# A state-space and layer-norm stage: loops unrolled, tables in halves, moments taken by ScalarE

## The reference, cut to what matters

```
dt  = exp(log_dt);  A = -exp(inv_A_real) + 1j * A_imag;  dtA = A * dt
Cc  = B * C * (exp(dtA) - 1) / A
K[c, h, l] = 2 * real(sum_n Cc[c, h, n] * exp(dtA[h, n] * l))       # c < 16, h < 128, n < 64, l < 1024
h   = K                                                            # 16 x 128 tokens of 1024 features
xn  = (h - mean(h)) / sqrt(var(h) + 1e-5)                          # over the 1024 features of a token
h   = h + attention(xn);   h = h + ffn(layernorm(h))
```

## Time and profile before

| | us |
|---|---|
| median of 3 runs | 2087.96 (2087.77 to 2090.44) |
| the profiled execution | 2088.66 |
| its span, first to last instruction | 2086.7 |
| PE busy in the span | 1896.5 (91%) |
| DVE busy | 1163.6 (56%) |
| POOL busy | 618.0 (30%) |
| ACT busy | 612.7 (29%) |
| mean granted TensorE clock | 0.978 |

### The profile page before, as it was taken

The page is one execution under the profiler, slowest core; times in us unless marked ns, Lnnn a source line. Parts: engine busy times, 40 slices in busy tenths (PEclk is TensorE's granted clock), DMA queues, the critical chain, the costliest instruction groups (busy, mean ns, idle before and its releaser), DMA issues.

```text
span 2086.7 us, 31307 instructions
## 1 busy us (share of the span) xinstructions
PE 1896.5 (91%) x13212; PEld 1029.0 (49%) x13212; DVE 1163.6 (56%) x1476; ACT 612.7 (29%) x869; POOL 618.0 (30%) x261
## 2 busy tenths in 40 slices
PE   0377699999999898878999999999999999999999
PEld 0367576666656554444554444444444444444444
DVE  8998547777777778855644544444444444210111
ACT  2154324334333334421112333333333333200000
POOL 2675013343333334433310322232232232011101
PEclk9998799999999999999999999999999999999999
DMA  2022211111132112135441321322322232533441
GB/s 90 10 71 60 65 35 33 39 39 35 29 94 72 27 36 60 57 104 194 154 147 61 119 94 62 101 91 61 101 91 77 85 101 72 195 120 116 142 142 41
DMA packets 99812, 173.32 MB, mean 83 GB/s; under 512 B 13984, under 2 KB 75168, under 8 KB 91744
## 3 DMA queue, kind: packets, MB, share of 16 engines
q1 hardware_dynamic: 99680, 171.41, 25.7%
HBM read 114.22 MB, written 56.11 MB: 82 GB/s over the span
## 4 chain that ended last, share of the span: by engine, by line
PE 73%; DVE 8%; POOL 2%; issue 2%; ACT 2%; DMA 1%; SPq 1%; ACTq 0%; DVEq 0%
PE acc L1194 14%; PE acc L1123 14%; PE acc L1124 14%; PE ps_p L930 3%; PE ps_p L931 3%; PE ps_p L932 3%; PE acc L1044 3%; PE acc L1045 3%; PE acc L1046 3%; PE ps_t L957 2%; PE ps_p L946 2%; PE ps_p L948 2%; PE ps_p L947 2%; DVE prob L1464 2%; PE ps_l L1139 2%
## 5 line engine op out<-in xcount | busy, mean ns | idle before, releaser
L1123 PE MATMUL acc<-x_hi,q_f 128*128 128x512 f16 x1376 | 522.0, 379 | 0.0
L1124 PE MATMUL acc<-x_lo,q_f 128*128 128x512 f16 x1376 | 521.5, 379 | 0.0
L1194 PE MATMUL acc<-down_levels,hid_parts 128*128 128x512 f16 x1376 | 300.1, 379 | 0.0
L890 POOL TENSOR_TENSOR prob<-prob,mx 128x1024 f32<-128x1024 f32 x64 | 121.4, 1897 | 421.9 <-DVE mx L1471 421.9
L1123 PEld LDWEIGHTS acc<-x_hi,q_f 128*128 128x128 f16 x1376 | 134.5, 98 | 174.8 <-issue 17.8
L899 POOL TENSOR_SCALAR q_f<-q_raw 128x2048 f16<-128x2048 int32 x22 | 121.1, 5504 | 316.3 <-PE acc L1124 315.4
L1194 PEld LDWEIGHTS acc<-down_levels,hid_parts 128*128 128x128 f16 x1376 | 133.2, 98 | 163.1 <-issue 5.0
L1124 PEld LDWEIGHTS acc<-x_lo,q_f 128*128 128x128 f16 x1376 | 134.7, 98 | 156.9
L930 PE MATMUL ps_p<-x_hi,w_qk 128*128 128x512 f16 x512 | 196.8, 384 | 0.0
L931 PE MATMUL ps_p<-x_lo,w_qk 128*128 128x512 f16 x512 | 196.0, 383 | 0.0
L932 PE MATMUL ps_p<-x_hi,w_qk 128*128 128x512 f16 x512 | 195.7, 382 | 0.0
(11 more groups left out here) (284 smaller groups left out, 3081.5 us busy)
## 6 DMA issues: line engine op xcount, KB each, us to landing
q_raw<-in_gu_q SPq DMA_DIRECT2D x22, 1024.0 KB, 7.1
hidden_parts<-hidden SPq DMA_DIRECT2D x42, 512.0 KB, 3.5
hid_parts<-hidden_parts SPq DMA_DIRECT2D x15, 1376.0 KB, 6.7
down_raw<-in_down_q SPq DMA_DIRECT2D x22, 512.0 KB, 5.1
w_raw<-in_w_qk SPq DMA_DIRECT2D x8, 1024.0 KB, 4.8
h_tokens<-n_tok SPq DMA_DIRECT2D x16, 512.0 KB, 3.8
o_parts<-ot SPq DMA_DIRECT2D x32, 256.0 KB, 2.3
wv_raw<-in_w_o SPq DMA_DIRECT2D x8, 1024.0 KB, 4.8
```

Source lines behind the costliest of these rows:

```text
L890: nc.gpsimd.tensor_tensor(prob[s % 2][p][:], prob[s % 2][p][:], bc(mx[p][:], H, 2), ALU.subtract).then_inc(s_sub[p], 1)
L1123: nc.tensor.matmul(acc[u % 2][:, m, :], lev, x2_hi[:, k, tok], start=(k == 0), stop=False)
L1124: last = nc.tensor.matmul(acc[u % 2][:, m, :], lev, x2_lo[:, k, tok], start=False, stop=(k == KT - 1))
L1194: last = nc.tensor.matmul(acc[n % 2][:, b, :], parts[n % 3][:, at], levels[:, i, b * CH:(b + 1) * CH], start=(i == 0 and part == 0), stop= ...
```

## The change

- **Loops.** `run`, the register loops and the semaphores that start as free are gone; each engine's list is straight-line code over `k`, with the semaphores counted per unit.
- **Head.** Phases, sines, table products and `a1`, `a2` are made in two halves of 64 channels (`heads(k)`). `mag` is made by 32 exponentials of 128 x 128 on ACT, one per step, with the step as their scale: POOL's L197 goes. Both table products are DVE's: POOL's L200 goes. The second half of `a1`, `a2` is made in three pieces within the first units.
- **Moments.** `tokens` and a new `squares` give sums with `accum_out`; DVE makes `minus_mean` (`mean`); `deviation` takes the root of the mean square. `bn_stats` and `bn_aggr` go.
- **Order.** Lags and the order within each engine change, and so do the places of `find_tops`, `find_big`, `find_scale`, `exchange` and the weights' high and low halves.

The core of the diff (the head's arithmetic, the semaphores' names and the buffers are left out):

```diff
@@ sync
-            with sp.Fori(0, VIS) as n:
...
-            first.exchange(sp, 0)
+            for u in range(UNITS):
+                sp.wait_ge(s_tok, u + 1)
+                sp.dma_start(h0_dram[:, channels(u), :], tok[u % 2][:]).then_inc(s_out[u % 2], 16)
+                if u == UNITS - 5:
+                    first.exchange(sp, 0)
@@ gpsimd
+            for u in range(UNITS):
+                pool.wait_ge(s_tab, 1 + 2 * u // UNITS)
+                pool.wait_ge(s_trig, 2)
+                if u >= 2:
+                    pool.wait_ge(s_mm, u - 1)
...
+                pool.wait_ge(s_a, 2 if u < UNITS // 2 else 4)
@@ tensor
+            def product(u):
+                pe.wait_ge(s_v, u + 1)
...
-            run(pe, [(5, to_features), (1, product), (2, to_tokens)])
+            for k in range(UNITS + 3):
+                if each(0, k):
+                    product(k)
+                if each(1, k):
+                    to_tokens(k - 1)
+                if each(3, k):
+                    to_features(k - 3)
@@ scalar
+            for k, step in enumerate(STEPS_OF):
+                last = nc.scalar.activation(mag[:, :, k], t[2][:], ACT.Exp, scale=float(step))
...
+            def columns(u):
+                act.wait_ge(s_mm, u + 1)
...
+            def tokens(u):
...
+                nc.scalar.activation(tok[u % 2][:].rearrange("p (i j) -> p i j", j=P), pt[:], ACT.Identity,
+                                     accum_out=total[u % 2][:]).then_inc(s_tok, 1)
+            def squares(u):
+                act.wait_ge(s_mean, u + 1)
...
+                nc.scalar.activation(nrm[u % 2], tok[u % 2][:], ACT.Square, bias=minus_mean[u % 2][:],
+                                     accum_out=square[u % 2][:]).then_inc(s_sq, 1)
...
+            for k in range(UNITS + 3):
+                if each(0, k):
+                    columns(k)
+                if each(2, k):
+                    normalise(k - 2)
+                if each(1, k):
+                    tokens(k - 1)
+                if each(3, k):
+                    high(k - 3)
+                if each(1, k):
+                    squares(k - 1)
+                    deviation(k - 1)
+                if k in (UNITS - 1, UNITS):
+                    act.wait_ge(s_v, UNITS)
+                    first.high(nc, act, 0, k - UNITS + 1)
@@ vector
+            def mean(u):
+                dve.wait_ge(s_tok, u + 1)
...
+                ts(minus_mean[u % 2][:], total[u % 2][:], -1.0 / D, None, ALU.mult).then_inc(s_mean, 1)
...
+            for k in range(-1, UNITS + 3):
+                if each(2, k):
+                    inverse(k - 2)
+                if each(-1, k):
+                    second_factor(k + 1)
+                    second_power(k + 1)
+                if each(1, k):
+                    mean(k - 1)
+                if each(-1, k):
+                    power(k + 1)
+                if 1 <= k < 4:
+                    rotations(1, k - 1)
+                if k == UNITS - 9:
                     first.find_tops(nc, dve, chain)
                     first.find_big(nc, dve, chain, 0)
+                if k == UNITS - 4:
                     first.find_scale(nc, dve, chain, 0)
+                if each(3, k):
+                    low(k - 3)
+                if k in (UNITS, UNITS + 1):
+                    first.low(nc, dve, 0, k - UNITS)
```

More of the change, by code:

```diff
@@ L81 @@
 TAB = 2 * TI + TJ
-LAG = 6
+STEPS_OF = [P * k for k in range(TI)] + [TJ * k for k in range(TI)] + list(range(TJ))
+HALF_H = H // 2
 def ssm_and_norm(nc, ssm, cr, ci, h0_dram, xn_hi, xn_lo, ident, w_first, wv_first, b_first, first, rooms):
@@ L123, in ssm_and_norm @@
         nrm = [nrm0[:], mag_room[:, 3, :]]
-        stats = [sb(f"n_stats{s}", [P, 2, 6]) for s in two]
-        mv = [sb(f"n_mv{s}", [P, 2]) for s in two]
-        std = [sb(f"n_std{s}", [P, 1]) for s in two]
+        total, square, minus_mean, std = ([sb(f"n_{n}{s}", [P, 1]) for s in two] for n in ("total", "square", "mean", "std"))
         rs = [sb(f"n_rs{s}", [P, 2]) for s in two]
@@ L147, in four, with channels, heads, each @@
             return room.rearrange("p (h a b) -> p h a b", h=UH, b=n)
[L149 to L172, removed]
+        def channels(u, start=0, end=UH):
+            return slice(u * UH + start, u * UH + end)
+        def heads(k):
+            return slice(k * HALF_H, (k + 1) * HALF_H)
+        def each(lag, k):
+            return 0 <= k - lag < UNITS
         @block.sync
@@ L256, in _ @@
+            last.then_inc(s_mag, 1)
             act.wait_ge(s_const, 3 + 15)
@@ L258, in _ @@
             quarter = half[5]
[L259 to L288, removed]
-            run(act, [(2, columns), (4, deviation), (3, tokens), (4, normalise), (5, high)])
-            first.high(nc, act, 0, 0)
-            first.high(nc, act, 0, 1)
+            for k in two:
+                hs = heads(k)
+                act.wait_ge(s_phase, k + 1)
+                nc.scalar.activation(tab1[:, hs, 0:2 * TI], tab1[:, hs, 0:2 * TI], ACT.Sin, scale=-TWO_PI, bias=quarter[:])
+                nc.scalar.activation(tab1[:, hs, j0], tab1[:, hs, j0], ACT.Sin, scale=half[1][:], bias=half[3][:])
+                nc.scalar.activation(tab2[:, hs, i], phase[:, hs, i], ACT.Sin, scale=TWO_PI)
+                nc.scalar.activation(tab2[:, hs, j1], phase[:, hs, j1], ACT.Sin, scale=half[1][:])
+                nc.scalar.activation(tab2[:, hs, j0], tab2[:, hs, j0], ACT.Sin, scale=half[2][:], bias=half[4][:]).then_inc(s_trig, 1)
@@ new lines, in squares, with deviation @@
+            def squares(u):
+                act.wait_ge(s_mean, u + 1)
+                act.wait_ge(s_tab, 2)
+                if u >= 2:
+                    act.wait_ge(s_trn, u - 1)
+                nc.scalar.activation(nrm[u % 2], tok[u % 2][:], ACT.Square, bias=minus_mean[u % 2][:],
+                                     accum_out=square[u % 2][:]).then_inc(s_sq, 1)
+            def deviation(u):
+                act.wait_ge(s_sq, u + 1)
+                nc.scalar.activation(std[u % 2][:], square[u % 2][:], ACT.Sqrt, scale=1.0 / D, bias=eps[:]).then_inc(s_std, 1)
@@ new lines, in normalise, with high @@
+            def normalise(u):
+                act.wait_ge(s_rs, u + 1)
+                nc.scalar.activation(nrm[u % 2], tok[u % 2][:], ACT.Identity, scale=rs[u % 2][:, 0:1], bias=rs[u % 2][:, 1:2]).then_inc(s_nrm, 1)
+            def high(u):
+                act.wait_ge(s_trn, u + 1)
+                nc.scalar.activation(xn_hi[:].rearrange("p k (c h) -> p k c h", h=H)[:, :, :, channels(u)],
+                                     pn[:].rearrange("p k (c h) -> p k c h", h=UH), ACT.Copy).then_inc(s_hi, 1)
@@ L333, in _ @@
+            chain.after(nc.vector.tensor_copy(t[6][:], t[3][:]))
             ts(t[8][:], t[6][:], MAGIC, MAGIC, ALU.add, ALU.subtract).then_inc(s_turn0, 1)
@@ L412, in moments @@
-            def moments(n, s):
-                dve.wait_ge(s_tok[s], n + 2)
-                chain.mark(nc.vector.bn_stats(stats[s][:, 0, :], tok[s][:, 0:512]))
-                chain.mark(nc.vector.bn_stats(stats[s][:, 1, :], tok[s][:, 512:D]))
-                apart(dve, s_passed, (s_dve, chain.now()))
-                nc.vector.bn_aggr(mv[s][:], stats[s][:].rearrange("p a b -> p (a b)")).then_inc(s_mv[s], 1)
-            def inverse(n, s):
-                dve.wait_ge(s_std[s], n + 1)
-                chain.after(nc.vector.reciprocal(rs[s][:, 0:1], std[s][:]))
-                nc.vector.scalar_tensor_tensor(rs[s][:, 1:2], mv[s][:, 0:1], -1.0, rs[s][:, 0:1], ALU.mult, ALU.mult).then_inc(s_rs[s], 1)
@@ new lines, in rotations @@
+            def rotations(k, part):
+                hs = heads(k)
+                e_re, e_im = tab1[:, hs, 0:TI], tab2[:, hs, 0:TI]
+                a_, b_ = bc(a[:, hs], TI, 2), bc(b[:, hs], TI, 2)
+                if part == 0:
+                    chain.mark(tt(a1[:, hs, :], a_, e_re, ALU.mult))
+                    chain.after(tt(at[:, hs, :], b_, e_im, ALU.mult))
+                if part == 1:
+                    tt(a1[:, hs, :], a1[:, hs, :], at[:, hs, :], ALU.add).then_inc(s_a, 1)
+                    dve.wait_ge(s_a, 2 * k + 1)
+                    chain.mark(tt(a2[:, hs, :], b_, e_re, ALU.mult))
+                if part == 2:
+                    chain.after(tt(at[:, hs, :], a_, e_im, ALU.mult))
+                    tt(a2[:, hs, :], a2[:, hs, :], at[:, hs, :], ALU.subtract).then_inc(s_a, 1)
+                    dve.wait_ge(s_a, 2 * k + 2)
@@ new lines, in _, with second_factor @@
+            dve.wait_ge(s_mag, 1)
+            tables(0)
+            dve.wait_ge(s_tab, 1)
+            for part in range(3):
+                rotations(0, part)
+            tables(1)
+            dve.wait_ge(s_tab, 2)
+            dve.wait_ge(s_c, 32)
+            def second_factor(u):
+                s, hs = u % 2, channels(u, CUT, UH)
+                if u >= 2:
+                    dve.wait_ge(s_mm, u - 1)
```

(33 more changed lines are left out.)

170 lines of the change are left out of this document (67 added, 103 removed).

## The result

| | before | after |
|---|---|---|
| median, us | 2087.86 (4 runs) | 2112.07 (2110.09 to 2112.97, 4 runs) |
| ratio | | 1.0112, 95% interval 1.0094 to 1.0129 |
| the profiled execution, us | 2088.66 | 2111.57 |
| mean granted TensorE clock | 0.978 | 0.975 |
| first DVE line of `layer` starts, us | 237.58 | 260.16 |

The change makes the kernel slower by 1.1%, some 24 us. In the two traces the next stage starts 22.6 us later; what follows it lasts 1849.6 us instead of 1849.1.

What follows compares the result with a forecast made beforehand. Bound before: DVE's list, with DVE and POOL excluding each other; after: a ring of 10.7 us a unit. Head -9.6, units and wait +21 (as written), drain -9.6 gave +21.5 and 2109.5 us, range 2090 to 2123.

Steps and rivals of the forecast that it cites:

- Only the stage's end counts: Everything after the stage starts behind a barrier, so only the moment the stage ends can move the time.
- The head: Up to the first power: without POOL's L197, L324 and L363 shorten; first power at 71.0 instead of 80.6, gain 9.6 us.
- The ring: Each unit: product, ACT's `columns`, `normalise`, `tokens`, then DVE's `mean` and `power`; product + 5.2 us, 10.7 us a unit.
- way back: In each unit, from the product's end through ACT, `mean`, POOL and `power` to the next product's start: 5.2 us.
- `rotations` and `find_big` fit in: In DVE's list: pieces of `rotations`, 1.4 us each in three units, and `find_big`, 3.2, stay hidden in the unit.
- The clock in the ring: TensorE's product took 3.74 or 5.37 us by granted clock; after 5.2 us pauses a slow one was taken, 5.5 us.
- the clock stays up: Rival in the units: products at 3.8 us make rings of 9.0; 2088 us, no change; chance 0.09.
- The wait for the scale: `find_scale` in DVE's list behind `power(13)`, `exchange` behind `tokens(11)`: DVE stands for 11 us, adding 7.0 us.
- `mean` does not wait for the port: DVE's 128 x 1 `mean` takes 0.16 us beside POOL; the rival that it waits: 2121 us, chance 0.12.
- The drain: From the last power to the stage's end, ACT's list the bound: 25.7 us instead of 35.3, -9.6.
- The sum's split: Stage change by parts: -9.6 in the head, +21 in units and wait, -9.6 in the drain, given as +21.5 us.
- the first products: After `power(0)` at 71.0: products end at 76.9 and 80.7, and `power(2)` ends near 85.5 us.

Runs made afterwards that it cites:

- e1: The changed kernel with one swap in DVE's list, `power(k+1)` ahead of `mean(k-1)`: 2089.95 us, 1.0005 to the kernel before.
- e5: The changed kernel with `exchange` behind `tokens(8)`, `to_tokens(k-1)` ahead of `product(k)` on PE and `tokens(k-1)` ahead of `columns(k)` on ACT: 2067.95 us, 0.9900 to before.
- e8: e5 with `power(k+1)` ahead of `mean(k-1)` in DVE's list as well: 2070.74 us, 0.9912 to the kernel before.
- e4: The changed kernel with 12 unused matmuls of `ident` by itself added in each pause of TensorE, order kept: 2095.29 us, 1.0032 to the kernel before.
- e3: The changed kernel with e1's swap and `exchange` moved from behind `tokens(11)` to behind `tokens(8)`: 2080.27 us, 0.9967 to the kernel before.
- e7: The changed kernel with VectorE's moments (two `bn_stats`, a `bn_aggr`) in the place of `mean`, `squares` gone: 2125.31 us, 1.0173 to the kernel before.

## Why the prediction was right

The forecast of 2109.5 us (2090 to 2123, slower) against 2112.07. By its steps:

- **Only the stage's end counts.** Right: 1849.6 and 1849.1 us follow it.
- **The head**, first power at 71.0 instead of 80.6: measured 69.9. The tables began at 46.2 us (46.8 in the prediction, 61.7 before). The saving is POOL's two table operations that no longer exclude DVE: L324's 11.34 us became two of 2.29, and L363's 8.89 became 0.29. Another 0.9 us, which the prediction doesn't have, came from the start: DVE's first instruction began at 3.95 instead of 4.83 us. No experiment was made on the head.
- **The ring**, product + 5.2 = 10.7 us: measured 10.58 in the unit shown (5.47 + 5.11), 11.0 on average (powers from 83.1 to 233.1 are 150.0 us; without the 17.8 of `find_scale` 132.2 for 12). Over these twelve the product took 5.7 us on average, not 5.5, since three took 6.55 to 6.78. The way back took 5.3 on average, not 5.2: it was 5.1 in most, but 6.4 at 88.7 us and 6.1 at 154.2. There the prediction's sentence that `rotations` and `find_big` fit in was wrong. They pushed `second_power` behind the end of the product, into POOL's operations, where it took 2.94 and 2.96 us instead of 1.22. The product's mean matmul, over the units, was 355 ns; one takes 275 ns in the products of 3.74 us, at a granted clock of 1.00, and the slowest took 583:

```profile
L202 PE MATMUL ssm_ps<-phase,magnitude 128*128 128x128 f32 x480 | 83.3, 355 | 115.4 <-DVE magnitude L441 115.4
```

- **The ring as the cause.** Shown by e1 and by e5 and e8, which cut it at two places. e5 keeps all of ACT's new work and runs 44 us faster.
- **The clock in the ring.** Shown by e4: 1.6 us of each unit. The term was taken rightly, and the rival "the clock stays up" would have been 2088; with filled pauses it is 2095. The reading of the earlier trace rows that it rests on passed over one product of the first units, at 94.91 us: it began 3.3 us after the one before it had ended, and was slow all the same. So the length of the pause alone does not tell which product is slow:

```profile
94.91 5.47 PE L228 MATMUL ssm_ps<-phase,magnitude 128*128 128x128 f32 x32 [2.40 <-DVE magnitude L410]
```

- **The wait for the scale**, 11 us of standing and 7.0 us of time: 11.4 and 7.8.
- **`mean` does not wait for the port.** `mean` ran at 0.153 to 0.155 us in all 16 units, at 146.94 in the middle of POOL's L186. The row of L422 would have misled. The Trainium skill (SBUF — State Buffer, Who interferes with whom) says that a VectorE instruction with at most one SBUF input, outside the two-port modes, does not contend with GpSimd, and that one with two SBUF inputs contends with a GpSimd instruction that reads SBUF. `mean` and `power` agree with it. The section also says that TENSOR_SCALAR can enter a two-port mode, in which it would contend; in these 16 units it did not.
- **The drain**, 25.7: measured 25.7.
- **The sum's split is wrong in the text.** The prediction writes "+21 in the units and the wait" beside 160.6 and 119.9 us, whose difference is 40.7; its parts as written don't add up to +21.5, while -9.6, +40.7 and -9.6 do. Measured: -10.7, +43.3 and -9.5. The stage's end was summed from the absolute times and is not touched by it.
- **Some of the closeness is luck.** Against the sum the head was 1.1 us shorter and the first products 1.2 (from the first power to the third 13.3 instead of 14.5 us), while the rings and the wait were 3.9 longer (150.0 instead of 146.1).

The expectation that failed most was e1's, of 7.5 to 8.2 us a unit, and e3's with it. Having cut a ring of one unit I did not look for the one of two units through the same wait. e5's was 3 us too low, and e4's and e7's missed by 1 us. What is left open is why e5's units are still 8.4 us long. Waits for POOL are in them, and PE's order may take part; no run here parts them.

## What to carry to other kernels

When the order of steps on in-order engines is rewritten, go round each ring: from a step to the next unit's same step, over every engine that it passes, counting what stands ahead in each list. A wait on another unit's late step, put in front of the step that feeds the matrix engine, costs the whole way round each time, however idle the engines are. Here the two swaps of e5 were worth 1.75%, 37 us (1.0075 to 0.9900), while moving the layer norm's moments to another engine was worth 3.5, within the noise. And a transfer's round trip (half a kilobyte written to DRAM and read back to all partitions: 12.4 us before, 12.7 after) belongs several units ahead of what reads it.

## What the runs showed that was not expected

- Twelve added matmuls a unit made the kernel 17 us faster, since the product behind a pause of 3.4 us took 5.47 us and behind one of 0.7 us 3.84 (e4).
- A product after a pause can take 6.4 to 6.8 us and not only the 5.4 of the earlier trace rows: 6.78 at 115.70 in the change, every second one in e7. No run shows what decides between the two.
- In e1 three of DVE's operations behind `mean` were stretched to 1.65, 2.94 and 1.74 us by POOL, whose work a product had released: 3.7 of the 9.6 us that lead to the next power. `squares` and the square root took 2.2.
